# A vision tower's first attention turn: the engines' instruction lists written out in another order

## The chip, the cores and the metric

The kernel runs on 1 core of a Trainium2 chip. The metric is the device time of one execution in microseconds (us). PE is TensorE, DVE is VectorE, ACT is ScalarE, POOL is GpSimd, and SP is the engine that issues the DMAs.

## The reference

The input x is 64 x 128 x 64 complex coefficients (the last axis is their real and imaginary part); a diagonal state-space kernel makes 64 blocks of 128 tokens by 1024 features from it (`tok_h` in the kernel). Then every block goes through one attention layer and one feed-forward layer, each behind a layer norm and with a residual:

```python
h = _L0_tok_ref(log_dt, x, B, inv_A_real, A_imag, 1024)     # [64, 128, 1024]
h = h + _L0_attn_ref(_layernorm(h), wq, wk, wv, wo)          # 32 heads of 32, 8 kv heads, rotary, causal
h = h + _L0_ffn_ref(_layernorm(h), W_base, b_base, lora_A, lora_B, router_W, router_b, prior, active)
```

The feed-forward layer is `x @ W_base.T + b_base` plus four low-rank experts weighted by a softmax router. With 128 tokens the token-selection part of the attention allows every causal position, so the attention is a plain causal softmax.

## The kernel before

The program has a first part (`token_kernel`, up to about 235 us) that makes `tok_h` and stores it to HBM, and a second part (`tower`) that works through 64 blocks in a software pipeline of turns. In turn b the engines do the attention of block b (eight steps u of four heads), the q, k and v products of block n = b + 1, the first layer norm of block m = b + 2, the output product of block p = b - 1, and the feed-forward of block f = b - 2. Turn -1 and turn 0 have only the parts whose block exists: turn 0 has the attention of block 0, q, k and v of block 1 and the norm of block 2. From turn 2 on all parts are there.

Each engine has its own list of instructions, written out by hand in a function `turn(b, ...)` of its own (SP L1151, POOL L1293, ACT L1430, DVE L1646, PE L2015), and the lists meet only in semaphores. There is no planner. The steps of one attention step u are:

- `scores(u)` on PE (L2018): four matmuls into one of two PSUM banks; it waits for maxima(u - 2), which freed the bank.
- `maxima(u)` on DVE (L1649): four fused mask-and-minimum instructions that copy the scores to one of four SBUF buffers.
- `exps(u)` on ACT (L1433): four exponentials with row sums.
- `invert(u)` on DVE (L1662): two small instructions; `normalise(u)` on POOL (L1296); `probs_high(u)` on ACT (L1444) and `probs_low(u)` on POOL (L1301), the two fp16 halves; `turn_probs(u)` on SP (L1154), a transposing DMA.

The q, k and v products (`kv`, `q`, 72 matmuls of 512 columns per block) are followed by the rotation (`rope` on DVE L1676, its sum on POOL L1305), the high and low fp16 halves of the heads (`heads_high` on ACT L1457, `heads_low` on DVE L1703) and a transposing DMA (`turn_heads` on SP L1162). v has its halves in `v_hi` (ACT L1508) and `v_low` (DVE L1698).

Turn 0 also carries the last part of the weight preparation. `W_base` is turned in 16 jobs (J_B to J_B + 15 of the list, called 0 to 15 here). A job is four fp32 transpositions on PE (`turn`, L894) into one of three PSUM banks in rotation, a scaled high fp16 half on ACT (`high`, L713), and a low half on DVE (`low`, L821). The transposition of job j waits until the low half of job j - 3 has freed its bank (L914). Jobs 2u and 2u + 1 together are base(u) in what follows. Ahead of them stands `spread(2)` on PE and, on DVE, the scale of the matrix (`powers(2)`, L883), and once in turn 0 the sum of the router's priors (L887).

In the kernel before, turn 0 has the same code as every other turn, with hooks: ACT does the high halves of base(u) right behind exps(u) (`early(u)`, L771), DVE the low halves of base(u) right ahead of maxima(u + 1) (L1763 and on), and PE the transpositions of base(u) inside `scores(u)`:

```python
                    if u == 0 and not some(b):
                        prep.spread(pe, 2)
                    if not some(b):
                        prep.turn(pe, prep.jb + 2 * u, prep.jb + 2 * u + 2)
```

so that PE's order in turn 0 is scores(0), base(0), 21 of the 24 kv matmuls, scores(1), base(1), 3 kv and 18 q matmuls, scores(2), base(2), and so on; after scores(4) no products are left, and PE's list is scores and transpositions only. Turn 1 begins with scores(0) of block 1 and kv of block 2.

## Time and profile before

| | us |
|---|---|
| median of 3 runs | 2895.47 |
| lowest and highest of them | 2894.19, 2898.05 |
| the profiled execution's own time | 2895.14 |
| its span in the profile | 2893.2 |
| PE busy (share of the span) | 2799.6 (97%) |
| DVE, ACT, POOL busy | 82%, 66%, 68% |

The profiled execution took 1.9 us more than the span of its instructions. Times in the rows below count from the span's start. A row of a timeline has: start, length, engine, line, operation, output and input tile; in brackets the idle time of the engine just before it and what ended it. Turn 0 runs on PE from 262.7 us (scores(0)) to 303.0 us, turn 1 from there to 336 us.

### The profile page before, as it was taken

What the parts mean: (1) busy time and instruction counts of PE and PEld (TensorE: products, weight loads), DVE (VectorE), ACT (ScalarE), POOL (GpSimd) and SP (SyncE); (2) the same over time, 40 slices, a digit from 0 to 9 for tenths busy, and PEclk for the clock granted to TensorE, in tenths of its full rate; (3) what the DMA queues carried; (4) which work ended last, traced back from release to release, by engine and by line L of the source; (5) the groups of instructions that cost most, each with busy time, mean ns of one, the idle gap of its engine ahead of it and who ended that gap; (6) DMA issues with size and microseconds to landing.
All of it is one profiled execution on the core that took longest, in us unless ns stands there. A gap on an engine that the chain in (4) does not pass through costs nothing.

```text
span 2893.2 us, 61884 instructions
## 1 busy us (share of the span) xinstructions
PE 2799.6 (97%) x16932; PEld 1408.5 (49%) x16932; DVE 2366.2 (82%) x8776; ACT 1918.2 (66%) x5986; POOL 1970.2 (68%) x1730
## 2 busy tenths in 40 slices
PE   6788899999999999999999999999999999999997
PEld 5665444444444444444444444444444444444443
DVE  9987788888888888888888888888888888888784
ACT  8887766666666666666666666666666666666662
POOL 4542677777777776777777777777767777777763
PEclk9999899999999999999999999999999999999999
DMA  7884677666666666666666666666666666666763
GB/s 246 231 217 135 142 153 150 149 149 151 151 143 152 146 156 147 151 149 147 152 148 149 149 150 151 143 152 147 156 149 148 150 146 152 150 149 149 152 132 78
DMA packets 1220851, 442.64 MB, mean 153 GB/s; under 512 B 1167120, under 2 KB 1175568, under 8 KB 1220640
## 3 DMA queue, kind: packets, MB, share of 16 engines
q1 hardware_dynamic: 1220640, 440.69, 66.7%
q14 instruction: 183, 1.50, 0.2%
q8 instruction: 28, 0.46, 0.1%
HBM read 88.22 MB, written 67.11 MB: 54 GB/s over the span
## 4 chain that ended last, share of the span: by engine, by line
PE 89%; DVE 3%; DMA 3%; ACT 2%; issue 1%; POOL 1%; SPq 1%; DVEq 0%; ACTq 0%; POOLq 0%
PE bank_b L2068 44%; PE bank_a L2068 22%; PE bank_c L2068 11%; PE score L2031 4%; PE kps L581 2%; PE pv L2057 2%; DMA tok_h<-kout 2%; PE bank_b L2057 1%; PE bank_b L2227 1%; DMA xc<-in_x_dram 1%; PE pv L2160 1%; ACT kout L358 1%; ACT probs L1440 0%; PE bank_c L2121 0%; PE pv L2121 0%
## 5 line engine op out<-in xcount | busy, mean ns | idle before, releaser
L1440 ACT ACTIVATE probs<-probs,negmax 128x128 f32<-128x128 f32 x2016 | 777.3, 387 | 247.4 <-DVE negmax L1658 247.3
L1303 POOL TENSOR_TENSOR p_hl<-probs,p_hl 128x512 f16<-128x512 f32 x503 | 607.6, 1208 | 333.9 <-ACT p_hl L1449 331.4
L1299 POOL TENSOR_TENSOR probs<-probs,rsum 128x512 f32<-128x512 f32 x503 | 547.6, 1089 | 183.5 <-DVE rsum L1669 183.1
L1658 DVE CUSTOM_DVE_ANT_0 probs<-score,table,scal 128x128 f32<-128x128 f32 x2016 | 589.0, 347 | 78.1 <-issue 77.4
L2068 PE MATMUL bank_a<-qkv_hi,xt 128*128 128x512 f16 x2048 | 642.6, 380 | 2.0 <-DMA xt<-xy_hl 2.0
L2068 PE MATMUL bank_b<-b_hi,yt 128*128 128x512 f16 x1952 | 610.7, 379 | 0.0
L1449 ACT ACTIVATE p_hl<-probs 128x512 f16<-128x512 f32 x503 | 314.5, 625 | 417.8 <-POOL probs L1299 417.8
L1712 DVE TENSOR_TENSOR heads<-rope_a,heads 128x512 f16<-128x512 f32 x319 | 388.1, 1232 | 30.0 <-ACT heads L1470 29.9
L2068 PE MATMUL bank_a<-qkv_lo,xt 128*128 128x512 f16 x1024 | 389.7, 381 | 0.0
L1440 ACT ACTIVATION_READ_ACCUMULATOR probs<-probs,negmax 128x1 f32 x2016 | 376.5, 187 | 0.0
L2068 PE MATMUL bank_b<-o_hi,at_hi 128*128 128x512 f16 x992 | 376.4, 379 | 0.0
L2068 PE MATMUL bank_b<-o_lo,at_hi 128*128 128x512 f16 x992 | 376.4, 379 | 0.0
L2068 PE MATMUL bank_b<-o_hi,at_lo 128*128 128x512 f16 x992 | 376.4, 379 | 0.0
L2068 PE MATMUL bank_b<-b_lo,yt 128*128 128x512 f16 x976 | 370.2, 379 | 0.0
L2068 PE MATMUL bank_c<-qkv_hi,xt 128*128 128x512 f16 x1024 | 326.2, 380 | 0.0
L2068 PEld LDWEIGHTS bank_a<-qkv_hi,xt 128*128 128x128 f16 x2048 | 200.7, 98 | 223.1 <-issue 2.7
L2068 PEld LDWEIGHTS bank_b<-b_hi,yt 128*128 128x128 f16 x1952 | 190.6, 98 | 209.0
L1318 POOL TENSOR_TENSOR xy_hl<-xyn,xy_hl 128x1024 f16<-128x1024 f32 x125 | 266.4, 2131 | 26.3 <-ACT xyn L1484 21.3
L1470 ACT ACTIVATE heads<-rope_a 128x512 f16<-128x512 f32 x320 | 192.5, 620 | 90.9 <-POOL rope_a L1309 85.4
L1309 POOL TENSOR_TENSOR rope_a<-rope_a,rope_b 128x512 f32<-128x512 f32 (+1 forms) x192 | 208.8, 1088 | 40.1 <-DVE rope_b L1695 37.2
L2031 PEld LDWEIGHTS score<-kstack,stack 128*128 128x128 f16 x2016 | 152.5, 98 | 114.4 <-issue 2.5
L2031 PE MATMUL score<-kstack,stack 128*128 128x128 f16 x2016 | 195.6, 220 | 2.9 <-DVE negmax L1658 2.0
(311 smaller groups left out, 4590.2 us busy)
## 6 DMA issues: line engine op xcount, KB each, us to landing
hin<-tok_h SPq DMA_DIRECT2D x64, 512.0 KB, 3.2
r<-tok_h SPq DMA_DIRECT2D x64, 512.0 KB, 3.8
out_dram<-r SPq DMA_DIRECT2D x63, 512.0 KB, 3.0
tok_h<-kout SPq DMA_DIRECT2D x60, 512.0 KB, 6.1
probs_t<-p_hl SPq DMA_TRANSPOSE x512, 3.1
xc<-in_x_dram SPq DMA_DIRECT2D x32, 128.0 KB, 4.5
raw_a<-in_L_attn_wq_dram SPq DMA_DIRECT2D x4, 1024.0 KB, 9.2
raw_b<-in_L_attn_wo_dram SPq DMA_DIRECT2D x8, 512.0 KB, 4.8
```

The lines of the kernel that those rows point to most:

```text
L1299: TT(x, x, rsum[:, u % 4].unsqueeze(2).to_broadcast([P, GR, T]), ALU.mult).then_inc(s_norm, 1)
L1303: TT(p_hl[:, u % 2, 1], probs[:, u % 4], p_hl[:, u % 2, 0], ALU.subtract).then_inc(s_plo, 1)
L1309: TT(rope_a[:, 0:hs], rope_a[:, 0:hs], rope_b[:, 0:hs], ALU.add).then_inc(s_rope2, 1)
L1318: TT(xy_hl[:, 1], xyn[:, :], xy_hl[:, 0], ALU.subtract).then_inc(done, 1)
L1440: ins = A(probs[:, u % 4, g], probs[:, u % 4, g], ACT.Exp, bias=negmax[:, u % 4, g:g + 1], scale=-1.0, accum_out=sums[:, u % 4, g:g + 1])
L1449: A(p_hl[:, u % 2, 0], probs[:, u % 4], ACT.Copy).then_inc(s_phi, 1)
L1470: A(dst, src, ACT.Copy).then_inc(s_hhi, 1)
L1658: ins = V.tensor_tensor_reduce(probs[:, u % 4, g], score[u % 2][:, g], mask, col(U_SC), 3e38, ALU.add, ALU.min, negmax[:, u % 4, g:g + 1])
L1712: TT(dst, full_.unsqueeze(2).to_broadcast([P, 8, 2, HD]), hi, ALU.subtract).then_inc(s_hlo, 1)
L2031: ins = MM(score[u % 2][:, g], stack[:, h // 8, h % 8], kstack[:, par, u], start=True, stop=True)
L2057: ins = MM(half_out[a][32 * k:32 * k + 32].rearrange("p g t -> p (g t)"), v[:, 1 - par, (4 * a + k) * HD:(4 * a + k + 1) * HD], probs_t[:, ...
L2068: ins = MM(bank, x(c), w[:, c, cols], start=(c == 0 and i == 0), stop=(c == KC - 1 and i == 2))
```

## The change

No part of the computation is added or removed. Turn 0 gets a list of its own on all five engines, each behind `if attention and not some(b)` with a `return` at its end, and the hooks for b = 0 go away. In the new lists PE does scores(0), the spread and scores(1) first, then alternates half products of 12 matmuls (kv in two, q in four halves), base(u) and scores(u + 2). ACT does exps(u + 1) ahead of the high halves of base(u), and its other work of a step between the two. DVE does maxima(u + 1) and invert(u) ahead of the low halves of base(u). The new helpers `base` on ACT, DVE and PE issue the same instructions as the hooks did; `base_scale` and `priors` hold the lines that stood in `early`. On POOL each probs_low(u) comes right behind normalise(u), with the rotation sums and the norm between. On SP the transposing DMA of the normalised rows comes after that of probability tile 5 instead of tile 4.

```diff
--- before.py
+++ after.py
@@ -768,8 +768,6 @@
                 base_sums(6, NO)
             if b == -1 and k == "last":
                 Prep.high(act, MID + 4, J_B)
-            if b == 0 and k != "norm" and k != "last":
-                Prep.high(act, J_B + 2 * k, J_B + 2 * k + 2)
 
         @staticmethod
         def dve_tools(dve):
@@ -879,16 +877,19 @@
                     columns(2)
                 if b == -1 and k == "end":
                     low(MID + 4, J_B)
-                if b == 0 and k == 0:
-                    powers(2)
-                    TS(col(U_B), col(P_B), 2.0 ** -14 / XS, None, ALU.mult).then_inc(s_scal[2], 1)
-                if b == 0 and k == 5:
-                    dve.wait_ge(s_pr, 2)
-                    TT(keep["lp"][:, :], prs[:, :], prior[:, :], ALU.add)
-                if b == 0 and isinstance(k, int):
-                    low(J_B + 2 * k, J_B + 2 * k + 2)
-
-            return select, first_columns, begin, after, early
+
+            def base_scale():
+                powers(2)
+                TS(col(U_B), col(P_B), 2.0 ** -14 / XS, None, ALU.mult).then_inc(s_scal[2], 1)
+
+            def priors():
+                dve.wait_ge(s_pr, 2)
+                TT(keep["lp"][:, :], prs[:, :], prior[:, :], ALU.add)
+
+            def base(u):
+                low(J_B + 2 * u, J_B + 2 * u + 2)
+
+            return select, first_columns, begin, after, early, base_scale, priors, base
 
         @staticmethod
         def turn(pe, j0, j1):
@@ -1177,6 +1178,30 @@
                         sp.wait_ge(prep.base_row, 1)
                     sp.dma_start_transpose(dst, src).then_inc(s_st[c], 16)
 
+                def turn_rows():
+                    sp.wait_ge(s_xlo, m + 1)
+                    sp.wait_ge(s_q, n * 2 + 2)
+                    sp.dma_start_transpose(xt[:, :, :, :].rearrange("p a c t -> p (a c) t"),
+                                           xy_hl[:, :, :].rearrange("p a k -> p (a k)")).then_inc(s_xt, 16)
+
+                if attention and not some(b):
+                    turn_heads(b, 3)
+                    turn_probs(b, 0)
+                    turn_probs(b, 1)
+                    turn_heads(n, "k")
+                    turn_probs(b, 2)
+                    sp.wait_ge(s_xhi, m + 1)
+                    load_h(m + 1)
+                    turn_probs(b, 3)
+                    turn_heads(n, 0)
+                    turn_heads(n, 1)
+                    turn_probs(b, 4)
+                    turn_probs(b, 5)
+                    turn_rows()
+                    turn_heads(n, 2)
+                    turn_probs(b, 6)
+                    return
+
                 if rest:
 
                     await_(sp, s_out, (p - 1) * 16)
@@ -1320,6 +1345,29 @@
                 def shift_of(c):
                     pool.wait_ge(s_bn2, c * 4 + 4)
                     scale_shift(mean2, var2, rstd2, shift2, s_rstd2, c)
+
+                if attention and not some(b):
+                    normalise(b, 0)
+                    probs_low(b, 0)
+                    normalise(b, 1)
+                    probs_low(b, 1)
+                    rope(0)
+                    normalise(b, 2)
+                    probs_low(b, 2)
+                    pool.wait_ge(s_bn1, m * 4 + 4)
+                    scale_shift(mean1, var1, rstd1, shift1, s_rstd1, m)
+                    normalise(b, 3)
+                    rope(1)
+                    probs_low(b, 3)
+                    low(s_xhi, m + 1, s_xlo)
+                    normalise(b, 4)
+                    probs_low(b, 4)
+                    normalise(b, 5)
+                    probs_low(b, 5)
+                    rope(2)
+                    normalise(b, 6)
+                    probs_low(b, 6)
+                    return
 
                 if finish:
                     shift_of(f)
@@ -1470,8 +1518,53 @@
                     A(dst, src, ACT.Copy).then_inc(s_hhi, 1)
 
                 def early(k):
-                    if isinstance(b, int) and b in (-1, 0):
+                    if isinstance(b, int) and b == -1:
                         prep.act_early(act, b, k, probs[:, 2:4].rearrange("p a g t -> p (a g t)"))
+
+                def norm1():
+                    act.wait_ge(s_rstd1, m * 2 + 2)
+                    A(xy_hl[:, 0], hin[:, :], ACT.Identity, bias=shift1[:, 0:1], scale=rstd1[:, 0:1])
+                    A(xyn[:, :], hin[:, :], ACT.Identity, bias=shift1[:, 0:1], scale=rstd1[:, 0:1]).then_inc(s_xhi, 1)
+
+                def turned_v():
+                    act.wait_ge(s_kv, n + 1)
+                    A(v_hi[:, 1 - par], bank_a[1][:, HKV * HD:2 * HKV * HD], ACT.Copy, scale=LSHIFT).then_inc(s_vhi, 1)
+
+                def base(u):
+                    prep.high(act, prep.jb + 2 * u, prep.jb + 2 * u + 2)
+
+                if attention and not some(b):
+                    exps(0)
+                    exps(1)
+                    base(0)
+                    probs_high(b, 0)
+                    exps(2)
+                    probs_high(b, 1)
+                    heads_high("k")
+                    base(1)
+                    exps(3)
+                    turned_v()
+                    probs_high(b, 2)
+                    base(2)
+                    exps(4)
+                    norm1()
+                    probs_high(b, 3)
+                    base(3)
+                    exps(5)
+                    heads_high(0)
+                    heads_high(1)
+                    probs_high(b, 4)
+                    base(4)
+                    exps(6)
+                    probs_high(b, 5)
+                    base(5)
+                    exps(7)
+                    heads_high(2)
+                    probs_high(b, 6)
+                    base(6)
+                    heads_high(3)
+                    base(7)
+                    return
 
                 if attention:
                     exps(0)
@@ -1633,7 +1726,7 @@
 
         @block.vector
         def _(dve):
-            select, first_columns, begin, after, early_of = prep.dve_tools(dve)
+            select, first_columns, begin, after, early_of, base_scale, priors, base = prep.dve_tools(dve)
             token_vector(dve, select, first_columns)
             V = nc.vector
             TS, TT, STT = V.tensor_scalar, V.tensor_tensor, V.scalar_tensor_tensor
@@ -1747,8 +1840,49 @@
                     STT(r[:, par, cut], low_rank[i], col(U_L), r[:, par, cut], ALU.mult, ALU.add).then_inc(s_lev, 1)
 
                 def early(k):
-                    if isinstance(b, int) and b in (-1, 0):
+                    if isinstance(b, int) and b == -1:
                         early_of(b, k)
+
+                if attention and not some(b):
+                    maxima(0)
+                    base_scale()
+                    heads_low(b, 3)
+                    maxima(1)
+                    invert(b, 0)
+                    base(0)
+                    maxima(2)
+                    invert(b, 1)
+                    rope(0)
+                    base(1)
+                    heads_low(n, "k")
+                    maxima(3)
+                    invert(b, 2)
+                    v_low()
+                    dve.wait_ge(s_hin, m * 16 + 16)
+                    half_stats(hin, 0, stats1, s_bn1)
+                    half_stats(hin, 1, stats1, s_bn1)
+                    spread(stats1, mv1, mean1, var1, marks[:, 2:3], s_bn1, s_rstd1, m)
+                    base(2)
+                    maxima(4)
+                    invert(b, 3)
+                    rope(1)
+                    base(3)
+                    maxima(5)
+                    invert(b, 4)
+                    heads_low(n, 0)
+                    heads_low(n, 1)
+                    priors()
+                    base(4)
+                    maxima(6)
+                    invert(b, 5)
+                    rope(2)
+                    base(5)
+                    maxima(7)
+                    heads_low(n, 2)
+                    invert(b, 6)
+                    base(6)
+                    base(7)
+                    return
 
                 early("start")
                 if finish:
@@ -2030,10 +2164,6 @@
                         h = u * GR + g
                         ins = MM(score[u % 2][:, g], stack[:, h // 8, h % 8], kstack[:, par, u], start=True, stop=True)
                     ins.then_inc(s_score, 1)
-                    if u == 0 and not some(b):
-                        prep.spread(pe, 2)
-                    if not some(b):
-                        prep.turn(pe, prep.jb + 2 * u, prep.jb + 2 * u + 2)
 
                 def attend(a):
 
@@ -2121,6 +2251,35 @@
                     MM(low_rank[j], zt[:, :], keep["lbs"][:, j * 512:(j + 1) * 512],
                        start=True, stop=True).then_inc(s_lo, 1)
 
+
+                def base(u):
+                    prep.turn(pe, prep.jb + 2 * u, prep.jb + 2 * u + 2)
+
+                if attention and not some(b):
+                    scores(0)
+                    prep.spread(pe, 2)
+                    scores(1)
+                    kv(0, 4)
+                    base(0)
+                    scores(2)
+                    kv(4, 8)
+                    base(1)
+                    scores(3)
+                    q(0, 0, 4)
+                    base(2)
+                    scores(4)
+                    q(0, 4, 8)
+                    base(3)
+                    scores(5)
+                    q(1, 0, 4)
+                    base(4)
+                    scores(6)
+                    q(1, 4, 8)
+                    base(5)
+                    scores(7)
+                    base(6)
+                    base(7)
+                    return
 
                 if attention:
                     scores(0)
```

## Rows read from the trace of the kernel before

**Rows 1.** The page, section 4: the chain that ended last, by engine.
```profile
PE 89%; DVE 3%; DMA 3%; ACT 2%; issue 1%; POOL 1%; SPq 1%; DVEq 0%; ACTq 0%; POOLq 0%
```

**Rows 2.** Stretches: length, busy PE PEld DVE ACT POOL, PEclk, DMA share, GB/s.
```profile
262.70:303.40 40.70, 28.36 (x174) 18.48 (x175) 32.78 (x127) 30.48 (x87) 21.00 (x20) 0.82 0.48 95
303.40:338.50 35.10, 31.02 (x180) 14.13 (x178) 25.83 (x108) 23.38 (x80) 21.88 (x21) 0.97 0.61 131
338.50:390.00 51.50, 51.50 (x290) 24.16 (x291) 42.15 (x177) 35.46 (x121) 36.63 (x35) 0.97 0.69 152
```

**Rows 3.** Timeline of PE: turn 0's end, turn 1's start, turn 2's start.
```profile
298.65 1.06 PE L924 MATMUL wt<-const,raw_a 128*128 128x128 f32 x4
302.13 1.09 PE L924 MATMUL wt<-const,raw_a 128*128 128x128 f32 x4 [2.42 <-DVE b_lo L826]
303.01 0.63 PE L2031 MATMUL score<-kstack,stack 128*128 128x128 f16 x4
303.43 0.64 PE L2068 MATMUL bank_a<-qkv_hi,xt 128*128 128x512 f16 x1
...
338.46 0.39 PE L2068 MATMUL bank_a<-qkv_hi,xt 128*128 128x512 f16 x1 [1.99 <-DMA xt<-xy_hl]
```

**Rows 4.** Waits in turn 1 (us in total, times, longest).
```profile
PE score L2031 <- DVE negmax L1658: 2.0, 2, 1.5
PE bank_a L2068 <- DMA xt<-xy_hl: 2.0, 1, 2.0
```

**Rows 5.** Timeline of DVE in turn 0: maxima, own steps, low halves.
```profile
266.88 1.41 DVE L826 SCALAR_TENSOR_TENSOR b_lo<-wt,scal,b_hi 128x512 f16<-128x512 f32 x2 [0.76 <-ACT b_hi L721]
269.09 0.35 DVE L1658 CUSTOM_DVE_ANT_0 probs<-score,table,scal 128x128 f32<-128x128 f32 x1 [0.79 <-issue]
...
281.45 0.42 DVE L1700 SCALAR_TENSOR_TENSOR v_lo<-bank_a,v_hi 128x256 f16<-128x256 f32 x1
...
284.35 0.16 DVE L1667 TENSOR_TENSOR share<-sums,small 128x4 f32<-128x4 f32 x1 [0.80 <-ACT probs L1440]
...
284.93 1.41 DVE L826 SCALAR_TENSOR_TENSOR b_lo<-wt,scal,b_hi 128x512 f16<-128x512 f32 x2 [0.20 <-ACT b_hi L721]
286.26 0.34 DVE L1658 CUSTOM_DVE_ANT_0 probs<-score,table,scal 128x128 f32<-128x128 f32 x1
...
287.35 1.29 DVE L1712 TENSOR_TENSOR heads<-rope_a,heads 128x512 f16<-128x512 f32 x2
...
295.44 1.09 DVE L887 TENSOR_TENSOR lp<-prs,prior_row 128x4 f32<-128x4 f32 x1
...
302.56 0.35 DVE L1658 CUSTOM_DVE_ANT_0 probs<-score,table,scal 128x128 f32<-128x128 f32 x1
...
306.02 1.41 DVE L826 SCALAR_TENSOR_TENSOR b_lo<-wt,scal,b_hi 128x512 f16<-128x512 f32 x2 [2.29 <-ACT b_hi L721]
```

**Rows 6.** Timeline of ACT in turn 0: exponentials, high halves, own steps.
```profile
278.62 0.37 ACT L1508 ACTIVATE v_hi<-bank_a 128x256 f16<-128x256 f32 x1
...
285.37 1.23 ACT L1523 ACTIVATE xy_hl<-hin,shift,rstd 128x1024 f16<-128x1024 f32 x1
...
287.63 0.62 ACT L1449 ACTIVATE p_hl<-probs 128x512 f16<-128x512 f32 x1
...
303.76 0.40 ACT L1440 ACTIVATE probs<-probs,negmax 128x128 f32<-128x128 f32 x1 [0.95 <-DVE negmax L1658]
...
305.32 1.24 ACT L721 ACTIVATE b_hi<-wt,scal 128x512 f16<-128x512 f32 x2
```

**Rows 7.** Timeline of POOL in turn 0: sum of a rotation, normalising, low part.
```profile
271.51 0.73 POOL L1309 TENSOR_TENSOR rope_a<-rope_a,rope_b 128x256 f32<-128x256 f32 x1 [14.72 <-DVE rope_b L1695]
...
301.11 1.04 POOL L1299 TENSOR_TENSOR probs<-probs,rsum 128x512 f32<-128x512 f32 x1 [1.70 <-DVE rsum L1669]
302.89 1.16 POOL L1303 TENSOR_TENSOR p_hl<-probs,p_hl 128x512 f16<-128x512 f32 x1 [0.74 <-ACT p_hl L1449]
```

**Rows 8.** The page, section 6: a DMA transposition, count, us to landing.
```profile
probs_t<-p_hl SPq DMA_TRANSPOSE x512, 3.1
```

## The prediction

> **What bounds the kernel now.** I read the chain that ended last first. PE holds 89% of it [rows 1], so time is lost only where PE stands still on that chain. Then the stretches [rows 2]: from 338.5 us on PE is busy in every microsecond, in turn 0 (262.7 to 303.4) for 28.36 of 40.70 us, in turn 1 for 31.02 of 35.10. So turn 0 leaves 12.3 us of gaps and turn 1 4.1 us, and whatever moves the first kv product of turn 2, at 338.46 [rows 3], moves the end of the kernel with it. The timeline of PE shows what the gaps of turn 0 wait for: the second of two transposition jobs needs a PSUM bank whose low half VectorE has not yet written [rows 3].
>
> That wait belongs to a ring of three engines. Its steps can be read in two timelines: maxima(7) starts at 302.56 and the exponentials of step 7 at 303.76 (1.20 later); those take until 305.32, where the high halves begin (1.56); the low halves begin at 306.02 (0.70) [rows 5, 6]; two low halves last 1.33, from 284.93 to the maxima at 286.26 [rows 5]. Together 4.79 us. In the kernel before, maxima(u+1) stands behind low(u), low(u) needs high(u), high(u) stands behind exps(u), and exps(u) needs maxima(u): one round per step. Six rounds from maxima(1) at 269.09 to maxima(7) at 302.56 take 33.5 us, 5.6 each: the bare 4.79 and 0.8 more. The other work of ScalarE stands between high(u) and exps(u+1), where ScalarE would wait for VectorE's low halves and maxima anyway, 2.5 us in each round.
>
> **The change, part by part.** No instruction is added or removed: the same 16 transposition jobs, 16 high and 16 low halves, exponentials, rotations and DMAs are issued in another order, so everything depends on the order. What looks like the gain is that exps(u+1) now comes before high(u). But maxima(u+2) now stands behind low(u) on VectorE, and on ScalarE high(u) stands behind exps(u+1), which needs maxima(u+1). The ring is as long as before; only its index has moved by one. What did change is what stands inside it: on ScalarE the other work of a step now lies between exps(u+1) and high(u), and while VectorE does low halves and maxima ScalarE has nothing it may start.
>
> (1) The start. scores(1) no longer stands behind two transposition jobs and 21 matmuls, and the low half that frees its bank precedes maxima(0) on VectorE. VectorE finished maxima(0), the scale and one low part of the heads before the idle 0.76 us that ends at 266.88, so at 266.12 [rows 5]; the new list has the same three ahead of maxima(1). So maxima(1) starts at about 266.2 instead of 269.09: a gain of 2.9.
>
> (2) The six rounds up to maxima(7). Each has 1.20 + 1.56 + 0.70 + 1.33 and its own extras; 0.1 of a ScalarE instruction overlaps with the next (two of 1.23 last 2.26 [rows 6]), so 0.62 counts 0.52 unless another engine waits for it.
> - base(0): no extras, 4.8.
> - base(1): probs_high(1) 0.62, POOL's probs_low 1.16 and rotation sum 0.73, ahead of heads_high(k) 0.52, and VectorE's heads_low 0.64 ahead of the maxima [rows 5 to 7]: 8.5.
> - base(2): v's high half 0.37 releases v's low half, with the row statistics behind it (281.45 until 283.55, 0.80 ahead of 284.35), 2.10 in all [rows 5, 6]. These replace the 0.70 of the high half, which is done beside them: 1.20 + 1.56 + 0.37 + 2.10 + 1.33 = 6.6.
> - base(3): the normalised rows, 2.26, and probs_high 0.52 [rows 6]: 7.6.
> - base(4): heads_high 0.52 and 0.62, heads_low 0.64, priors 1.09 [rows 5], then the low halves: 7.0. The priors are one 128x4 addition, and another 128x4 addition took 0.16 (284.35) [rows 5], so its 1.09 is mostly waiting, and may be less or more in another order: 0.9 less, or more by one POOL instruction, 1.2.
> - base(5): probs_high 0.52: 5.3.
>
> The Trainium skill, "SBUF — State Buffer", section "Who interferes with whom", says that a VectorE instruction with two SBUF inputs contends with a POOL instruction that reads SBUF, and the one that comes second blocks until the first ends. By it the priors cost 0.16 wherever POOL stands idle, and this round would be 6.1 and the final sum 9.9; by the row it is 7.0 and 10.8. Which holds depends on what POOL does just then.
>
> Sum 39.8 against 33.5: a loss of 6.3.
>
> (3) The tail. Before, turn 1 starts on PE 0.87 us after the start of maxima(7): its last transposition job needed low(6), which lay ahead of maxima(7). Now low(6) is behind maxima(7) and much else: 1.20 + 1.56, heads_high(2) 0.62, heads_low 0.64, invert(6) 0.38 (from 284.35 to 0.20 ahead of 284.93), POOL's normalise(6) 1.04, probs_high(6) 0.52, then 0.70 to the low half, which lasts 0.7, the last transposition job 0.88 and four score matmuls 0.42 (302.13 to 303.43) [rows 3, 5 to 7]. With four more hand-overs of 0.1 (an estimate; the 0.70 above holds one) 9.1 us. A loss of 8.2.
>
> First kv product of turn 1: 266.2 + 39.8 + 9.1 = 315.1 instead of 303.43, 11.7 later.
>
> (4) Queues. SP now issues the turned rows behind six turned probability tiles, and POOL makes their low part ahead of normalise(4). The last tile ahead of them can be issued when POOL has probs_low(5), which follows exps(6) in round base(5), some 9 us ahead of turn 1's kv product; two issues and a landing like the 3.1 us of a tile [rows 8] end before it. I cost this at nothing; if SP runs late, each microsecond past 315 adds one. load_h waits on SP for the normalised rows of base(3), with tile 3 and two heads behind it; tile 3 frees a buffer for probs_high(5) only, two rounds on. heads(k) lands in round base(2), some 30 us ahead of turn 1's scores(0); rope(2) feeds scores(4) of turn 1. All at nothing, under that cover.
>
> (5) Turn 1. Its gaps are waits for maxima, 2.0, and for the turned rows, 2.0 [rows 4], because VectorE enters it late: its last low halves end at 307.43 [rows 5], 4.0 after PE began. In the new order the low halves of jobs 13, 14 and 15 follow the one that releases PE, 0.7 each, while PE needs 1.3 for its job and the scores, so they end some 1.0 after PE began. At most the 3.0 between come back, at least nothing; no row is nearer to either end, and I take the middle, 1.5.
>
> (6) The clock. The granted clock was 0.82 over turn 0 and 0.97 over the 35.1 us of turn 1 [rows 2]: with levels of 2.4 and 1.2 GHz that is 0.06 x 35.1 = 2.1 us at the lower one, after turn 0's gaps, which cost 1.1. PE idles longer in the new turn 0. The bounds are nothing more, and all of kv(0,7) at the low level: the first of turn 1's matmuls shows 0.64 against 0.39 at full speed [rows 3], and 21 times these 0.25 are 5.2, less the 1.1 paid already 4.1. Turn 1's own row is nearest, the gaps ahead of it being like the new ones; I take 0.6.
>
> Sum: 11.7 - 1.5 + 0.6 = 10.8 us slower. The profiled execution took 2895.14, span 2893.2; the median shown is 2895.47, 0.3 above it. 2895.47 + 10.8 = 2906.3.
>
> That a ready instruction does not pass a waiting one is in the rows too: transposition job 14 was done at 299.71 [rows 3], yet ScalarE idled 0.95 us for the maxima before 303.76 and took job 14's high half only at 305.32, behind the exponentials [rows 6].
>
> **Rivals.**
> A, faster: the extras inside the ring are hidden, and it runs bare. Six rounds of 4.79 from 266.2 and a tail of 1.20 + 1.56 + 0.70 + 0.7 + 0.88 + 0.42 + 0.2 = 5.7 put turn 1 at 300.6, 2.8 early: 2892.7. It decides where each high half follows its exponentials within 0.1 us. For it: PE has 12.3 us of gaps to give. Against it: the lists put 0.5 to 3.7 us there. Only with all 4.0 us of turn 1's waits gone as well does it pass 0.2%: 2888.7. 10%, half of it with the waits gone.
> B: turn 1 absorbs more, all of its 4.0 us of waits [rows 4]: 11.7 - 4.0 = 7.7, 2903.2. For it: VectorE enters turn 1 less late. Against it: part of these waits are turn 1's own order. 15%.
> C: the clock stays low through turn 1's kv product, and POOL's instructions stretch one more VectorE step by 1.2: 11.7 - 1.5 + 4.1 + 1.2 = 15.5, 2911.0. For it: longer gaps. Against it: turn 1's 0.97. 15%.
> That the change does not do what it says is no rival here: every list is written out.
>
> **Numbers.** Forecast 60%, A 10%, B 15%, C 15%. The range goes from B, less 2.2 for rounds that come out shorter (0.9 of the priors and 1.3 of small estimates), up to C and 1 more: 2901 to 2912; A and the outer ends of B and C are left out. 0.2%, about what a measurement of this kernel can tell, is 5.8 us, so slower means above 2901.3: the forecast, C and two thirds of B, 0.85; within 0.2% the rest of B and half of A, 0.10; faster 0.05.
>
> **What would show it.** Right: maxima(1) at 266.2; maxima(2) to (7) 4.8 to 8.5 us apart, with base(1) the longest; ScalarE's idle before the exponentials near 2.5 us in every round; the last base transposition waiting 5 us or more, and turn 1's kv product near 315; from turn 2 on the same 51.5 us of 51.5. Wrong: maxima spaced by 5 us, or a high half ahead of its exponentials; turn 1's gaps under 1 us (B); turn 1's kv matmuls 0.43 apart beyond 3 us (C).

## The result and the profile after

The changed kernel takes 2904.9 us (median of 7 runs, 2901.66 to 2908.12) beside 2894.93 us for the kernel before, measured alongside; the ratio is 1.0037 with a 95% interval from 1.0028 to 1.0046. It is some 10.0 us slower; 2906.3 was forecast, between 2901 and 2912. The span of the profiled execution went from 2893.2 to 2904.1 us, 10.9 more.

The page of the changed kernel, section 4, answers to [rows 1]:

```profile
PE 88%; DVE 5%; ACT 3%; issue 2%; DMA 1%; POOL 1%; SPq 0%; DVEq 0%; ACTq 0%; POOLq 0%
```

DVE and ACT hold 8% of the chain of the whole kernel where they held 5%. The stretches say where. They are cut here at the first scores of turn 0 and at the first kv products of turns 1 and 2; columns as in [rows 2].

```profile
263.30:315.22 51.92, 31.82 (x174) 19.57 (x175) 32.01 (x129) 32.71 (x97) 21.43 (x20) 0.81 0.42 78
315.22:351.29 36.07, 31.98 (x178) 14.32 (x177) 24.18 (x104) 21.05 (x71) 21.24 (x20) 0.94 0.58 122
351.29:403.00 51.71, 50.38 (x294) 24.03 (x295) 42.89 (x177) 35.73 (x121) 37.07 (x35) 1.00 0.74 151
```

The kernel before, cut at the same events:

```profile
262.75:303.43 40.68, 28.39 (x174) 18.48 (x175) 32.79 (x127) 30.43 (x87) 21.02 (x20) 0.82 0.48 96
303.43:338.46 35.03, 30.95 (x178) 14.06 (x177) 25.76 (x108) 23.34 (x80) 21.81 (x21) 0.97 0.62 131
```

Turn 0 is 11.24 us longer (51.92 against 40.68). VectorE, ScalarE and POOL did the same work in it within 2.3 us each; PE stood still for 20.1 us instead of 12.3, and the same matmuls took 3.4 us longer, more of them at the lower clock (0.63 us a row instead of 0.39 in the timeline below). Turn 1 is 1.04 us longer. Waits between 262 and 314 us (total, times, longest):

```profile
PE wt L925 <- DVE b_lo L824: 20.0, 6, 6.2
ACT probs L1488 <- DVE negmax L1751: 14.6, 7, 2.9
DVE b_lo L824 <- ACT b_hi L721: 13.5, 5, 4.3
```

The last two lines are the ring: ScalarE waits for the maxima, and VectorE, whose next maxima stand behind its low halves, waits for the high halves. PE hangs on it, waiting for the low halves. PE's timeline answers to [rows 3, 4]; the last column is the idle time ahead and what ended it.

```profile
278.84 1.08 PE L925 MATMUL wt<-const,raw_a 128*128 128x128 f32 x4 [3.96 <-DVE b_lo L824]
...
305.81 1.91 PE L925 MATMUL wt<-const,raw_a 128*128 128x128 f32 x8 [4.02 <-DVE b_lo L824]
313.92 1.09 PE L925 MATMUL wt<-const,raw_a 128*128 128x128 f32 x4 [6.19 <-DVE b_lo L824]
315.22 0.63 PE L2198 MATMUL bank_a<-qkv_hi,xt 128*128 128x512 f16 x1
...
319.49 0.39 PE L2198 MATMUL bank_a<-qkv_lo,xt 128*128 128x512 f16 x1
...
321.88 0.39 PE L2165 MATMUL score<-kstack,stack 128*128 128x128 f16 x4
...
343.51 0.40 PE L2165 MATMUL score<-kstack,stack 128*128 128x128 f16 x4 [1.53 <-DVE negmax L1751]
348.93 0.38 PE L2165 MATMUL score<-kstack,stack 128*128 128x128 f16 x4 [0.49 <-DVE negmax L1751]
351.29 0.39 PE L2198 MATMUL bank_a<-qkv_hi,xt 128*128 128x512 f16 x1 [1.98 <-DMA xt<-xy_hl]
```

The last three are turn 1's waits: 2.0 us for maxima and 2.0 for the turned rows, exactly what [rows 4] shows of before. VectorE's timeline, where each maxima(u), u from 1 to 7, begins, with the priors, the last low half and the maxima(1) of turn 1:

```profile
266.60 0.35 DVE L1751 CUSTOM_DVE_ANT_0 probs<-score,table,scal 128x128 f32<-128x128 f32 x1
...
271.40 0.35 DVE L1751 CUSTOM_DVE_ANT_0 probs<-score,table,scal 128x128 f32<-128x128 f32 x1
...
277.95 1.41 DVE L824 SCALAR_TENSOR_TENSOR b_lo<-wt,scal,b_hi 128x512 f16<-128x512 f32 x2 [4.35 <-ACT b_hi L721]
...
279.88 0.35 DVE L1751 CUSTOM_DVE_ANT_0 probs<-score,table,scal 128x128 f32<-128x128 f32 x1
...
286.39 0.35 DVE L1751 CUSTOM_DVE_ANT_0 probs<-score,table,scal 128x128 f32<-128x128 f32 x1
...
293.96 0.34 DVE L1751 CUSTOM_DVE_ANT_0 probs<-score,table,scal 128x128 f32<-128x128 f32 x1
...
298.58 1.12 DVE L887 TENSOR_TENSOR lp<-prs,prior_row 128x4 f32<-128x4 f32 x1
...
300.94 0.34 DVE L1751 CUSTOM_DVE_ANT_0 probs<-score,table,scal 128x128 f32<-128x128 f32 x1
...
306.25 0.35 DVE L1751 CUSTOM_DVE_ANT_0 probs<-score,table,scal 128x128 f32<-128x128 f32 x1
...
315.76 0.75 DVE L824 SCALAR_TENSOR_TENSOR b_lo<-wt,scal,b_hi 128x512 f16<-128x512 f32 x1 [0.32 <-ACT b_hi L721]
...
322.31 0.35 DVE L1751 CUSTOM_DVE_ANT_0 probs<-score,table,scal 128x128 f32<-128x128 f32 x1 [3.76 <-issue]
```

The starts are 4.80, 8.48, 6.51, 7.57, 6.98 and 5.31 us apart, 39.65 in all; the 4.35 us of waiting in the second round is for base(1)'s high halves. From the last maxima to turn 1's kv product are 8.97 us. Four rows of ScalarE in one round show why its high halves come late: it idles 2.62 us for the maxima, then runs the exponentials and probs_high, and only then base(5).

```profile
298.28 1.24 ACT L721 ACTIVATE b_hi<-wt,scal 128x512 f16<-128x512 f32 x2
302.14 0.40 ACT L1488 ACTIVATE probs<-probs,negmax 128x128 f32<-128x128 f32 x1 [2.62 <-DVE negmax L1751]
...
303.70 0.61 ACT L1497 ACTIVATE p_hl<-probs 128x512 f16<-128x512 f32 x1
304.22 1.24 ACT L721 ACTIVATE b_hi<-wt,scal 128x512 f16<-128x512 f32 x2
```

### The profile page after: what moved, and what is told of

Read it like the earlier page. It is cut to its first block, busy times and chain, and to the rows that moved or that the text cites. A ratio compares the mean times of both kernels' runs of the same rounds, so it can differ in the third digit from the quotient of the medians.

```text
span 2904.1 us, 61884 instructions
## 1 busy us (share of the span) xinstructions
PE 2798.7 (96%) x16932; PEld 1408.6 (49%) x16932; DVE 2362.1 (81%) x8776; ACT 1918.1 (66%) x5986; POOL 1968.9 (68%) x1730
## 4 chain that ended last, share of the span: by engine, by line
PE 88%; DVE 5%; ACT 3%; issue 2%; DMA 1%; POOL 1%; SPq 0%; DVEq 0%; ACTq 0%; POOLq 0%
PE bank_b L2198 43%; PE bank_a L2198 22%; PE bank_c L2198 11%; PE score L2165 4%; PE kps L581 2%; PE pv L2187 2%; PE bank_b L2187 1%; PE bank_b L2386 1%; PE pv L2319 1%; DVE z L506 1%; DVE z L507 1%; DMA tok_h<-kout 1%; PE pv L2251 0%; PE bank_c L2251 0%; ACT probs L1488 0%
## 5 line engine op out<-in xcount | busy, mean ns | idle before, releaser
L1805 DVE TENSOR_TENSOR heads<-rope_a,heads 128x512 f16<-128x512 f32 x319 | 387.9, 1232 | 34.0 <-ACT heads L1518 33.9
```

The lines of the kernel that those rows point to most:

```text
L1805: TT(dst, full_.unsqueeze(2).to_broadcast([P, 8, 2, HD]), hi, ALU.subtract).then_inc(s_hlo, 1)
```

## The experiments

The theory is the ring: maxima(u+1), exps(u+1), high(u), low(u), maxima(u+2). Against it stands that TensorE's new list (early scores, dense products in halves) costs the time, or that ScalarE and VectorE are simply full. Ratios are to the kernel before, measured alongside each time; the table gives, for the profiled executions, the time from the first scores of turn 0 to turn 1's kv, from there to turn 2's kv, and the granted clock over the latter.

```
kernel               ratio [95%]               turn 0   turn 1  clock
before               1                          40.68    35.03   0.97
after                1.0037 [1.0028, 1.0046]    51.92    36.07   0.94
e1 TensorE's list    1.0006 [0.9997, 1.0015]    41.62    35.30   0.96
e2 lows moved        1.0015 [1.0006, 1.0024]    44.07    35.99   0.94
e3 tail              1.0028 [1.0018, 1.0039]    48.61    35.17   0.97
e4 base(1)           1.0033 [1.0021, 1.0045]    50.01    36.30   0.93
e5 ring open         0.9983 [0.9974, 0.9992]    35.44    34.97   0.97
e5 again             0.9983 [0.9974, 0.9992]    35.44    35.09   0.97
e7 turn 1's scores   1.0037 [1.0023, 1.0050]    52.34    34.76   0.97
e8 e5 and turn 1     0.9974 [0.9963, 0.9985]    35.86    34.27   0.95
```

One warning on the table's first column of times: the same code reached turn 0's first scores between 262.75 and 266.66 us after its start in these executions, so a span by itself carries up to 3.9 us that have nothing to do with the edits. The stretches don't.

**e1: TensorE's list alone.** The kernel before, with one part of the change, PE's:

```diff
-                    if not some(b):
-                        prep.turn(pe, prep.jb + 2 * u, prep.jb + 2 * u + 2)
...
+                if attention and not some(b):
+                    scores(0)
+                    prep.spread(pe, 2)
+                    scores(1)
+                    kv(0, 4)
+                    base(0)
+                    scores(2)
...
```

> The kernel before with TensorE's new order of turn 0 alone (scores(u+1) ahead of base(u), dense products in halves); VectorE, ScalarE, GpSimd and SyncE keep the lists of before. Theory (the ring of maxima, exponentials, high halves and low halves on VectorE and ScalarE sets turn 0): the ring is not made by TensorE's order, so turn 1's kv starts within 2 us of the 303.4 of before, by the durations of the rows at about +1.3, and the time is between 1 us below and 3 us above that of before. Rival 1 (TensorE's own new order costs the time: dense products in halves, base transpositions that are behind more scores): turn 1's kv starts at 311 to 315 as in the kernel after, and the time is 8 to 11 us above that of before.

Turn 0 took 41.62 us, 0.94 more than before; the time is 1.6 us above before's, and the interval holds no change at all. Its stretch of turn 0, columns as in [rows 2]:

```profile
263.20:304.82 41.62, 29.61 (x174) 17.94 (x175) 32.06 (x127) 30.54 (x87) 21.05 (x20) 0.87 0.46 93
```

In turn 0 TensorE's list, with the other engines' lists of before, costs 0.94 of the 11.24 us that the whole change costs there. The rest lies in the lists of the other engines.

**e2: the low halves one maxima later.** VectorE alone, six such moves:

```diff
                     invert(b, 0)
-                    base(0)
                     maxima(2)
+                    base(0)
                     invert(b, 1)
...
```

(base(1) to base(5) go behind maxima(3) to maxima(7) in the same way.)

> The kernel after, where on VectorE alone base(0) to base(5) each stand behind the next maxima but one: base(u) behind maxima(u+2) and not ahead of it. Theory (the ring maxima(u+1), exps(u+1), high(u), low(u), maxima(u+2)): this cuts the ring, since maxima(u+2) no longer waits for low(u), which waits for ScalarE's high(u) behind exps(u+1). VectorE's waits for high halves (13.5 us in 5 between 262 and 314 in the kernel after) fall by more than half, turn 1's kv starts about 8 us earlier than the 315.2 of after, at 305.5 to 309, and the time falls by 6 to 9 us, to 2896 to 2899. Rival 1 (TensorE's order sets it): the ring's rounds stay at 6.5 to 8.5 us and kv starts at 313 to 315; time within 2 us of after. Rival 2 (VectorE's and ScalarE's work in turn 0 fills them whatever its order): kv at 311 to 314, 1 to 4 us less than after.

Turn 0 fell by 7.85 us to 44.07, kv began at 307.20, and the time was 2897.8. VectorE's waits for high halves, over the same 262 to 314 us, and PE's for low halves:

```profile
PE wt L925 <- DVE b_lo L824: 14.2, 5, 4.7
...
DVE b_lo L824 <- ACT b_hi L721: 4.7, 5, 2.4
```

13.5 us became 4.7. So one edge of the ring, low(u) ahead of maxima(u+2), carried most of the loss; beyond the six moves (heads_low(k) comes ahead of base(1) by them) nothing was touched. That ScalarE and VectorE are simply full does not fit: with 33.78 and 32.78 us of work in it, a little more than in after, this turn 0 is 7.85 us shorter.

**e3: the tail.** On ScalarE and on VectorE:

```diff
                     exps(7)
+                    base(6)
                     heads_high(2)
                     probs_high(b, 6)
-                    base(6)
...
                     maxima(7)
+                    base(6)
                     heads_low(n, 2)
                     invert(b, 6)
-                    base(6)
```

> The kernel after, where base(6) stands right behind exps(7) on ScalarE and right behind maxima(7) on VectorE, so that heads_high(2), probs_high(6), heads_low(2) and invert(6) no longer stand between them. Theory: the 9.0 us from maxima(7) to turn 1's kv are a chain through base(6) and base(7) on ScalarE and VectorE, with that other work inside it; the tail becomes some 3 us shorter, kv starts at 311 to 313 where it starts at 315.2 in after, and the time is 1 to 3.5 us below after (part of the gain is lost where heads 2 and probabilities 6 come later for turn 1). Rounds 0 to 5 stay at the 39.6 us of after. Rival (the tail is TensorE's: its transpositions and the late scores(7) hold kv back): kv stays within 0.7 us of 315.2, and the time with it.

The six rounds summed to the same 39.65 us, and from maxima(7) at 308.42 to kv at 314.08 there were 5.66 instead of 8.97; the two ends in the timelines of VectorE and PE:

```profile
308.42 0.35 DVE L1751 CUSTOM_DVE_ANT_0 probs<-score,table,scal 128x128 f32<-128x128 f32 x1
...
314.08 0.63 PE L2198 MATMUL bank_a<-qkv_hi,xt 128*128 128x512 f16 x1
```

That 5.66 is the bare tail of 5.7 that rival A had priced from single rows. (kv at 314.08 misses the expected 311 to 313 because this execution reached turn 0 at 265.47, 2.17 us later than after's.) The time, 8.65 us above before's, can't be told from after's 10.0 by the intervals; the stretch can: 48.61 against 51.92. The 7.85 us of e2 and the 3.31 of e3 add up to 11.16 of the 11.24, but the two were not tried together.

**e4: base(1) ahead of exps(2).** ScalarE alone:

```diff
                     probs_high(b, 0)
+                    base(1)
                     exps(2)
                     probs_high(b, 1)
                     heads_high("k")
-                    base(1)
```

> The kernel after, where on ScalarE alone base(1) stands ahead of exps(2) and not behind probs_high(1) and heads_high(k). Theory (the ring): the second round, 8.5 us long in after because base(1) on ScalarE sat behind probs_high(1) and heads_high(k), becomes about 2 us shorter (6.5), the other rounds stay within 0.3 us, turn 1's kv starts 1.5 to 2.2 us earlier than the 51.92 us behind scores(0) that after shows, and the time is 1 to 2.5 us below after, 2902.5 to 2904 beside 2893.2 to 2895 of before. Rival (ScalarE's work fills the rounds whatever its order): the saving of round two comes back in rounds three to five, kv within 0.7 us of after's.

The maxima now start 4.79, 6.60, 6.50, 7.57, 6.98 and 5.30 us apart: the second round lost 1.88, the others nothing, and turn 0 lost 1.91. What the round lost is base(1)'s own halves: VectorE is done with them at 276.82 and then waits for the heads, which still come behind probs_high(1) and POOL's two steps.

```profile
279.28 0.69 DVE L1805 TENSOR_TENSOR heads<-rope_a,heads 128x512 f16<-128x512 f32 x1 [2.46 <-ACT heads L1518]
```

The time, 10.4 us above before's, can't show it: its interval reaches 3.5 us to either side, and turn 1, at a clock of 0.93, took 36.30.

**e5: the ring open.** TensorE's list of the change is kept; the other lists of turn 0 are put in another order:

```diff
 ScalarE
                     exps(0)
-                    exps(1)
                     base(0)
+                    exps(1)
                     probs_high(b, 0)
+                    base(1)
                     exps(2)
...
-                    base(1)
                     exps(3)
...
-                    exps(5)
                     heads_high(0)
                     heads_high(1)
+                    exps(5)
...
-                    exps(7)
                     heads_high(2)
-                    probs_high(b, 6)
                     base(6)
+                    exps(7)
+                    probs_high(b, 6)
 VectorE
                     base(1)
-                    heads_low(n, "k")
                     maxima(3)
                     invert(b, 2)
+                    heads_low(n, "k")
+                    maxima(4)
                     v_low()
...
-                    maxima(4)
...
-                    base(4)
                     maxima(6)
                     invert(b, 5)
+                    base(4)
```

On GpSimd rope(0) moves one place up, on SyncE the turned rows do.

> The kernel after with TensorE's list kept, and the other lists of turn 0 put in an order in which no low half stands ahead of a maxima that could run: ScalarE's base(u) right behind the exponentials it is due after or behind probs_high, VectorE's base(u) behind the maxima that follow, rope(0) of GpSimd one place earlier and the transposition of the rows one place earlier on SyncE. Theory (the ring, and not the dense products in halves or the early scores, is the cost): with the durations of the rows, and the ring open, turn 1's kv starts at 296 to 300 and turn 2's kv at 330 to 335, where they start at 303.4 and 338.5 in before and at 315.2 and 351.3 in after; the time is 3 to 8 us below that of before, 2887 to 2892. Rival 1 (the early scores and spread dense products cost by themselves, on TensorE): not earlier than before at turn 1's kv, 304 or later, and the time at or above before's. Rival 2 (the gain at turn 1's kv is given back in turn 1, which then waits for its rows and heads): kv of turn 1 at 296 to 300, but turn 2's kv at 337 or later, time within 2 us of before.

(The expectation's words go too far: base(0), base(1), base(3) and base(5) still stand ahead of the next maxima but one on VectorE. The ring is opened at base(0) and base(1), which ScalarE now does before the next exponentials, and at base(2) and base(4), which VectorE now does behind the maxima they held up; base(6) comes before the last exponentials. At base(3) and base(5) the edge is left.) Turns 0 and 1, columns as in [rows 2]:

```profile
263.61:299.05 35.44, 27.44 (x174) 17.69 (x175) 31.84 (x128) 31.04 (x94) 20.93 (x19) 0.93 0.52 109
299.05:334.02 34.97, 30.91 (x178) 14.02 (x176) 24.57 (x104) 22.29 (x73) 22.38 (x21) 0.97 0.63 132
```

The waits over the same 262 to 314 us:

```profile
PE wt L925 <- DVE b_lo L824: 7.9, 5, 2.8
ACT probs L1488 <- DVE negmax L1751: 5.8, 4, 2.3
DVE b_lo L824 <- ACT b_hi L721: 3.9, 3, 2.0
```

They were 20.0, 14.6 and 13.5 us in after. kv of turns 1 and 2 at 299.05 and 334.02, 2888.8 us beside 2893.2 for before: 0.9983, 0.9974 to 0.9992. Turn 0 is 16.5 us shorter than in after with the same instructions, and 5.2 shorter than in before. So TensorE's new list does not stand in the way of a shorter turn 0; the change's lists for ScalarE and VectorE do, and neither engine is full: VectorE's 31.84 and ScalarE's 31.04 us of work fit into 35.44. Whether the early scores are needed for e5's gain was not tried.

The same kernel was run again, beside e4, e7 and e8:

> The same kernel as e5, beside e4, e7 and e8 on one chip, as their measure. Turn 1's kv 35.4 us and turn 2's kv 70.4 us behind scores(0) of turn 0, as in e5 within 0.3 us where the granted clock is the same; time 3 to 8 us below before's in the same call.

Turn 0 took 35.44 us once more, turn 2's kv came 70.53 behind the first scores (70.41 in e5), and the ratio was the same.

**e7: why turn 1 gave nothing back.** The kernel after, PE in turn 1 alone:

```diff
+                first = isinstance(b, int) and b == 1
                 if attention:
                     scores(0)
+                if first:
+                    scores(1)
                 if qkv:
                     kv(0, 7)
-                if attention:
+                if attention and not first:
                     scores(1)
```

> The kernel after, where TensorE in turn 1 alone issues scores(1) ahead of kv and not behind its first seven eighths. It asks why turn 1 gave back nothing. Theory (turn 1's waits are made by TensorE's own list further on: VectorE waits for scores(2) and for q as well, not for the end of turn 0): maxima(1) of turn 1 starts 3 to 4 us earlier than its 322.3, maxima(2) stays within 0.5 us of its place behind scores(2), the waits of 1.5 and 0.5 us for negmax and of 2.0 us for the rows in turn 1 stay, kv of turn 1 to kv of turn 2 stays within 0.5 us of after's 36.07, and the time within 1 us of after. Rival (the late maxima(1), 3.8 us behind an idle VectorE, is what keeps turn 1's waits alive): the two waits for negmax go, turn 2's kv comes 1.5 to 2.0 us earlier, and so does the end.

maxima(1) came 2.82 us behind kv instead of 7.09, and yet the waits further on in PE's timeline are the same three:

```profile
345.97 0.40 PE L2165 MATMUL score<-kstack,stack 128*128 128x128 f16 x4 [1.53 <-DVE negmax L1751]
351.39 0.38 PE L2165 MATMUL score<-kstack,stack 128*128 128x128 f16 x4 [0.49 <-DVE negmax L1751]
353.76 0.39 PE L2198 MATMUL bank_a<-qkv_hi,xt 128*128 128x512 f16 x1 [1.99 <-DMA xt<-xy_hl]
```

The rival falls; kv itself came 0.42 later, behind the four score matmuls. Turn 1 did come out 1.31 us shorter than in after, more than the 0.5 expected; that is the clock, the last column but two of its stretch:

```profile
319.00:353.76 34.76, 30.67 (x174) 13.80 (x173) 23.95 (x103) 20.63 (x71) 21.24 (x20) 0.97 0.59 125
```

Length times granted clock is 33.7 here and 33.9 in after (36.07 x 0.94), and between 33.7 and 34.1 in every row of the table but the last (turn 1's gaps, some 4 us in all but the last, are counted in). Why the clock rose sooner here, this run does not say. The time did not move: 1.0037.

**e8: turn 1 with all early scores.** e5 and, in turn 1, on PE:

```diff
+                if first:
+                    scores(0)
+                    scores(1)
+                    kv(0, 7)
+                    scores(2)
+                    kv(7, 8)
+                    q(0, 0, 8)
+                    scores(3)
+                    attend(0)
...
```

> The open ring (e5) with, in turn 1 alone, TensorE's scores(1) ahead of kv, scores(2) ahead of its last eighth and scores(3) ahead of the attention products: all the early scores that turn 1's list can take without touching other engines. Theory: VectorE's maxima(1) to maxima(3) come earlier, but turn 1's rope on VectorE still waits for q, so that of the 4.0 us of waits in turn 1 about 1 us goes: kv of turn 1 to kv of turn 2 at 33.5 to 34.5 where e5 has 34.97, time 0.5 to 1.5 us below e5. Rival (turn 1's 4.0 us of waits are the lateness of maxima alone): kv to kv at 31 to 32, time 3 us or more below e5. Third (early scores do nothing in turn 1): within 0.4 us of e5.

Its turn 1 as a stretch, and the longest wait for maxima in PE's timeline:

```profile
298.96:333.23 34.27, 31.18 (x175) 14.12 (x173) 24.33 (x104) 21.89 (x73) 22.22 (x21) 0.95 0.62 131
```

```profile
325.47 0.40 PE L2165 MATMUL score<-kstack,stack 128*128 128x128 f16 x4 [0.64 <-DVE negmax L1751]
```

That wait fell from 1.52 in e5 to 0.64, and length times clock from 33.9 to 32.6, about the 1 us expected; both other waits stayed. 2887.2 us is the lowest of all kernels, 0.9974 of before, and 2.5 below e5 (2889.7, measured alongside) where 0.5 to 1.5 was expected. That the edit makes it faster than e5 is not settled: the intervals overlap, from turn 0's first scores to turn 2's kv it takes 70.13 us beside 70.41, and 2.6 us of the 3.6 between the two profiled spans (2885.2 and 2888.8) lie in a stretch near the end that the edit does not touch (25.91 against 28.54; see the last section).

## Why the prediction was right, and where it was not

Faster by more than 0.2% was given 0.05, slower 0.85; it was slower, by 10.0 where 10.8 was summed. By its steps (the times of after less 0.55, since its turn 0 began at 263.30 instead of 262.75):

- **The index of the ring only moves.** Held, and e2 shows it as cause: one edge taken away gives back 7.85 of 11.24 us.
- **(1) The start.** maxima(1) at 266.05 for 266.2.
- **(2) The rounds.** 4.80, 8.48, 6.51, 7.57, 6.98, 5.31 for 4.8, 8.5, 6.6, 7.6, 7.0, 5.3: 39.65 for 39.8. The extras read off single rows, POOL's part in base(1) included, were all inside the ring. e4 shows it for one round from the other side: with base(1)'s halves taken out, the maxima, the exponentials and the extras still hold it for 6.60.
- **The priors.** They took 1.12, the value by the row. POOL had begun an instruction 0.13 us ahead of them and ended it 0.02 us ahead of their end (298.45 + 1.23 = 299.68, against 299.70); the row is POOL's timeline in after:

```profile
298.45 1.23 POOL L1328 TENSOR_TENSOR p_hl<-probs,p_hl 128x512 f16<-128x512 f32 x1 [1.76 <-ACT p_hl L1497]
```

  In e2 the same addition fell between two instructions of POOL, one ended at 293.29 and one begun at 294.03, and took 0.15 (timelines of VectorE and POOL):

```profile
293.76 0.15 DVE L887 TENSOR_TENSOR lp<-prs,prior_row 128x4 f32<-128x4 f32 x1
...
291.89 1.40 POOL L1324 TENSOR_TENSOR probs<-probs,rsum 128x512 f32<-128x512 f32 x1 [0.31 <-DVE rsum L1762]
294.03 1.16 POOL L1328 TENSOR_TENSOR p_hl<-probs,p_hl 128x512 f16<-128x512 f32 x1 [0.74 <-ACT p_hl L1497]
```

  The Trainium skill, "SBUF — State Buffer", section "Who interferes with whom", has the later of the two blocked until the first ends. The trace agrees in both cases; only where POOL would stand was open.
- **(3) The tail.** 8.97 us for 9.1; e3 splits it into a bare 5.66 and 3.31 of other work. Turn 1's kv came 11.24 late for 11.7.
- **(4) The queues.** Nothing was owed: the turned rows of turn 1 were issued, by the timeline of SP's queue in after, well ahead of kv's 315.22, whose row shows no wait for them.

```profile
306.89 1.69 SPq L1184 DMA_TRANSPOSE xt<-xy_hl  x1
```

- **(5) Turn 1 gives 1.5 back.** This step failed: it gave nothing. The premise was that turn 1's waits arise because VectorE enters late. VectorE did come earlier, as forecast: its last low half ended at 316.51, 1.29 us after kv began, where it was 4.0 in before. In after it is early enough to stand idle 3.76 us before maxima(1), at 322.31, for PE's scores(1), issued only at 321.88 behind kv. In before maxima(1) already began at 309.48 behind scores(1) at 309.05, the same 0.43 later (timelines of PE and VectorE in before):

```profile
309.05 0.39 PE L2031 MATMUL score<-kstack,stack 128*128 128x128 f16 x4
309.48 0.35 DVE L1658 CUSTOM_DVE_ANT_0 probs<-score,table,scal 128x128 f32<-128x128 f32 x1
```

  From scores(1) to turn 2's kv it is 29.41 us in both. Turn 1's waits belong to its own order of work: e7 and e8 show that maxima alone don't remove them.
- **(6) The clock, 0.6.** It was 1.04, all that turn 1 grew by. kv ran at the lower level until 319.49, 4.27 us, where before it rose after some 2.6; with the 0.97 and 0.94 of the rows, 0.06 x 36.07 - 0.03 x 35.03 = 1.1. The prediction's upper bound, 4.1, was misread: 0.64 and 0.39 are lengths of single rows, but kv's products follow each other every 0.43 us at the lower level and every 0.22 above it, so that all 21 at the lower level cost 4.5, less 1.1: 3.4. With it C comes to 14.8 and 2910.3.
- **The signs.** Most came: the spacing of the maxima, 6.19 us of waiting for the last base transposition, kv near 315. Three did not come as named. ScalarE's idle before the exponentials was to be near 2.5 us in every round and was 1.48, 2.60, 2.93, 2.00, 2.62 and 2.00; the 2.5 leaves out that the second high half, some 0.5 us, runs beside the first low half. Turn 2 was to have PE busy throughout and had a gap (below). And a sign of rival C came: kv's matmuls stayed 0.43 apart for 4.27 us where 3 was the limit. Its price did not come: the clock cost 1.04 us more, not 3.4 or 4.1.

The steps up to turn 2's kv thus gave 11.24 + 1.04 = 12.28 for 10.8. Two differences behind it, which no step foresaw, brought the span's total back. From turn 2's kv to its first low-rank product (374.61 in before, 387.27 in after) the kernel before ran at the lower clock for a while (0.97 in [rows 2]) and after did not (1.00), but after had a gap of 1.33 us instead (50.38 busy of 51.71): together -0.17. The long middle, 2469.41 us from there to the stretch below, is the same to 0.01 us. A stretch of the same 140 matmuls near the end, in before and then in after (length, busy PE, PEclk, DMA share, GB/s):

```profile
2844.02:2872.54 28.52, 25.33 (x140) 0.94 0.32 78
```

```profile
2856.68:2883.53 26.85, 23.64 (x140) 1.00 0.33 82
```

1.67 us less, nearly all of it busy time (25.33 against 23.64) at full clock. With the 0.55 ahead of turn 0, 0.55 + 11.24 + 1.04 - 0.17 - 1.76 (the whole ending) = 10.9, the difference of the spans. So the sum of 10.8 met 10.9 between the two profiled executions only because terms that were 1.5 us too low in all (12.28 for 10.8) met -1.38 us of differences elsewhere (0.55 - 0.17 - 1.76). That it came so close is luck; that turn 0 loses some 11 us by its rounds and its tail is not.

## What to carry to other kernels

When a step is moved ahead on one engine, write down the cycle of waits through all engines before and after: if every edge is still there with its index shifted by one, nothing was pipelined, and whatever now stands between two edges has moved from idle time onto the cycle. Cutting one edge (the consumer's slot one step later, so that two rounds overlap) was worth more here than the reorderings inside it: e2's six moved lines gave 7.85 us of turn 0, e3's and e4's moves 3.31 and 1.91, and e5's order turned a loss of 10.0 us into a gain of 4.4. And before counting on a later stage to absorb a delay, check what its first wait is released by: if that is the delayed engine itself, the whole stage just moves along.

## What was not expected of the hardware

The granted clock differs between kernels far behind the edit, with the same instructions in the same order. The stretch of 140 matmuls near the end took 28.5 us at 0.94 in before and in both runs of e5 (28.54 in each), 26.85 us at 1.00 in after, and between 25.5 and 26.9 at 1.00 in the other kernels; it lies 2469 us behind turn 2's first low-rank product, the same to 0.3 us in all. The clock accounts for 1.7 us of the spread: PE is busy for 25.33 us at 0.94 and for 23.64 at 1.00. The rest, up to 1.3 us, is PE's wait for the turned rows in that stretch, 0.99 us in e1 and 1.28 and 1.34 in e7 and e8, where it is 2.25 to 2.32 in the others. So up to 3 us between two versions of this kernel arise in a part that neither touches, a third of what this change costs. What decides either is not settled: before and after both wait some 2.3 us there, and only before's clock falls behind it; no run here changed it alone.
